# One lane of the odd steps' y is evicted by VectorE instead of ScalarE in a displaced-convolution kernel

## The reference

```python
def _gn(v, G=32, eps=1e-5):
    g = v.reshape(B_, G, C_ // G, H_, W_)
    m = jnp.mean(g, axis=(2, 3, 4), keepdims=True)
    s = jnp.var(g, axis=(2, 3, 4), keepdims=True)
    return ((g - m) / jnp.sqrt(s + eps)).reshape(v.shape)
...
disp = _displace(x.reshape(B, P, cpp, h, w), off_int)
d = field[None] + sub[:, None, None, :]
kernel = jnp.exp(-jnp.sum(d * d, axis=-1) / (2.0 * SIGMA ** 2))
kernel = kernel / jnp.sum(kernel, axis=(1, 2), keepdims=True)
out = lax.conv_general_dilated(disp, kw, padding=[(c, c), (c, c)], feature_group_count=C)
...
x = x + _L0_conv_ref(_gn(x), L0_conv_offset)
```

## Time and profile before

| | us |
|---|---|
| median of 3 runs | 1216.74 |
| lowest and highest run | 1216.17, 1218.03 |
| the profiled execution, device time | 1216.96 |
| its span, first to last instruction | 1215.1 |
| PE busy | 1169.8 (96%) |
| PEld busy | 1127.1 (93%) |
| DVE busy | 995.5 (82%) |
| ACT busy | 697.5 (57%) |
| POOL busy | 660.9 (54%) |
| mean granted TensorE clock | 0.996 |

### The profile page before, as it was taken

The page is one execution under the profiler, slowest core; times in us unless marked ns, Lnnn a source line. Parts: engine busy times, 40 slices in busy tenths (PEclk is TensorE's granted clock), DMA queues, the critical chain, the costliest instruction groups (busy, mean ns, idle before and its releaser), DMA issues.

```text
span 1215.1 us, 110760 instructions
## 1 busy us (share of the span) xinstructions
PE 1169.8 (96%) x49408; PEld 1127.1 (93%) x49408; DVE 995.5 (82%) x1530; ACT 697.5 (57%) x595; POOL 660.9 (54%) x1478
## 2 busy tenths in 40 slices
PE   2899999999999999999999999999999999999996
PEld 2899999999999999999999999999999999999996
DVE  7688788888888888788888878878888888878863
ACT  3455655656656565665665665565565566566553
POOL 5455555556565555655556555555655556564551
PEclk9899999999999999999999999999999999999999
DMA  9799999999999999999999999999999999999955
GB/s 311 248 321 334 347 347 344 343 342 345 344 338 342 346 349 345 341 344 345 346 341 346 344 336 349 340 347 344 341 347 339 347 339 350 343 344 343 336 182 185
DMA packets 409765, 403.01 MB, mean 332 GB/s; under 512 B 16528, under 2 KB 409744, under 8 KB 409744
## 3 DMA queue, kind: packets, MB, share of 16 engines
q1 hardware_dynamic: 204944, 201.41, 51.3%
q10 hardware_dynamic: 204800, 201.36, 49.4%
HBM read 201.38 MB, written 201.33 MB: 331 GB/s over the span
## 4 chain that ended last, share of the span: by engine, by line
PE 94%; DVE 2%; issue 2%; POOL 1%; DVEq 0%; POOLq 0%
PE ps L604 59%; PE ps L615 31%; PE ps L596 4%; DVE ay L425 1%; DVE xin L460 1%; POOL norm L294 0%; POOL t_int L232 0%; POOL t_full L238 0%; POOL grid_i L212 0%; DVE xin L463 0%; POOL var L281 0%; POOL rstd L283 0%; DVEq L423 0%; DVE sub L379 0%; DVE tap L341 0%
## 5 line engine op out<-in xcount | busy, mean ns | idle before, releaser
L604 PE MATMUL ps<-ay,norm 32*128 32x128 f32 x24576 | 728.0, 273 | 0.9 <-DVE both L448 0.3
L604 PEld LDWEIGHTS ps<-ay,norm 32*128 32x128 f32 x24576 | 704.6, 187 | 11.0 <-issue 0.7
L549 ACT ACTIVATE y<-ps 128x1536 f32<-128x1536 f32 x256 | 369.7, 1444 | 420.3 <-PE ps L604 420.1
L441 DVE BATCH_NORM_STATS2 stats<-xin 128x6 f32<-128x512 f32 x768 | 475.7, 689 | 0.1
L615 PE MATMUL ps<-ax,y 64*64 64x64 f32 x24576 | 419.4, 220 | 7.8 <-issue 7.6
L615 PEld LDWEIGHTS ps<-ax,y 64*64 64x64 f32 x24576 | 383.8, 135 | 29.6 <-issue 8.6
L294 POOL TENSOR_SCALAR norm<-xin,rstd,bias 128x768 f32<-128x768 f32 x256 | 264.1, 1032 | 211.1 <-PE ps L604 187.6
L463 DVE TENSOR_TENSOR xin<-ps,xin 128x1024 f32<-128x1024 f32 x256 | 312.7, 1222 | 45.7 <-PE ps L615 45.7
L540 ACT ACTIVATE norm<-xin,bias,rstd 128x768 f32<-128x768 f32 x256 | 262.9, 1028 | 73.8 <-issue 73.5
L460 DVE TENSOR_TENSOR xin<-ps,xin 128x512 f32<-128x512 f32 x256 | 175.6, 686 | 150.1 <-PE ps L615 150.1
L274 POOL TENSOR_TENSOR mean_sq<-both 128x4 f32<-128x4 f32 x128 | 25.5, 199 | 218.6 <-DVE both L448 198.2
(11 more groups left out here) (54 smaller groups left out, 188.2 us busy)
## 6 DMA issues: line engine op xcount, KB each, us to landing
xin<-in_x_dram SPq DMA_DIRECT2D x512, 384.0 KB, 5.6
out_dram<-xin ACTq DMA_DIRECT2D x512, 384.0 KB, 6.2
off<-in_L_conv_offset_dram SPq DMA_DIRECT2D x1, 48.0 KB, 3.4
```

The lines of the kernel that those rows point to most:

```text
L441: nc.vector.bn_stats(stats[:, s // PAIR % RING, s % PAIR, n, :], xin[:, s].rearrange("p (g q) f -> p q f g", g=GROUPS)[:, n]).then_inc(bn_ ...
L549: nc.scalar.activation(y[:, v].rearrange("p k r a m -> p a (k r) m"), ps[:, v, :, 0:POS * P].rearrange("p a (n m) -> p a n m", m=32), ACT. ...
L604: last = nc.tensor.matmul(ps[:, v, a, P * k:P * (k + 1)], norm[rows, v, r, P * k:P * (k + 1)], ay[rows, k, r, :], start=(r == 0), stop=(r ...
```

## The change

A new function `copy_last_lane` on VectorE copies lane 3 of the odd step's y (384 columns, one bank) from PSUM to SBUF, in every even step, ahead of that step's `add_x`; in step 14 it stands behind `swap_rows`. ScalarE's copy in odd steps is cut to the lanes 0 to 2 (1152 columns); in even steps it stays as it is. A new semaphore `last_lane_ready` tells TensorE, which now waits for it as well before `x_products(1)`.

```diff
+        last_lane_ready = sem("last_lane_ready")
...
+            def copy_last_lane(t):
+                dve.wait_ge(y_done, t + 1)
+                nc.vector.tensor_copy(y[:, 1].rearrange("p k r a m -> p a (k r) m")[:, LANES - 1],
+                                      ps[:, 1, LANES - 1, 0:POS * P].rearrange("p (n m) -> p n m", m=32)
+                                      ).then_inc(last_lane_ready, PAIR)
...
                 if s == STEPS - PAIR and not tail:
                     swap_rows(c + 1)
+                if s % PAIR == 0:
+                    copy_last_lane(t + 1)
                 for part in range(ADDS):
                     add_x(t, s, part)
...
             def copy_y(t, v, first):
+                lanes = LANES - v
                 act.wait_ge(y_done, t + 1)
                 if not first:
                     act.wait_ge(x_done, ADDS * (t - 1))
-                nc.scalar.activation(y[:, v].rearrange("p k r a m -> p a (k r) m"),
-                                     ps[:, v, :, 0:POS * P].rearrange("p a (n m) -> p a n m", m=32),
+                nc.scalar.activation(y[:, v].rearrange("p k r a m -> p a (k r) m")[:, 0:lanes],
+                                     ps[:, v, 0:lanes, 0:POS * P].rearrange("p a (n m) -> p a n m", m=32),
                                      ACT.Copy).then_inc(y_ready, 1)
...
                 pe.wait_ge(y_ready, two)
+                pe.wait_ge(last_lane_ready, one)
                 pe.sem_inc(x_started, 1)
                 x_products(1)
```

## The result

The changed kernel took 1227.19 us (median of four runs, 1226.46 to 1227.47) against 1217.22 us for the kernel before beside it. The ratio is 1.0075, with a 95% interval of 1.0062 to 1.0088, so 7.5 to 10.7 us slower; the two medians lie 10.0 us apart. The forecast was 1224.8 us, in a range of 1219.5 to 1235. The profiled execution is 1226.46 us with a span of 1224.6 us, 9.5 us above the span of before.

A forecast was written before the change was run, and what follows sets the result against it. TensorE, 94% of the chain, was taken as the bound, with VectorE's L460 gating `sum_stats`. Terms +7.05 + 1.2 - 0.2 = +8.05 us on 1216.74 gave 1224.8 us, range 1219.5 to 1235.

The forecast's parts named there:

- The gate: VectorE's L460 releases TensorE's `sum_stats` 0.15 us after its end in all 126 pairs, without slack.
- The copy's duration: VectorE's new copy of 384 columns from PSUM takes 552 ns, with ends of 0.35 and 0.69 us.
- rival B: VectorE's copy runs at the rate of copies in SBUF, 0.35 us, giving 1220.6 us; chance 0.10.
- The usual pair: In 96 pairs the copy runs from +0.14 to +0.69, covered with 0.16 us to spare: cost 0.
- Rival A: Cover in usual pairs too thin: copy starts later or takes longer, L460 0.08 us late, 1235.5 us; chance 0.17.
- The swap pair: In 15 pairs with `swap_rows` the copy queues ahead of L460, which starts 0.47 us later: +7.05 us.
- The pair behind `values`: In 15 pairs the copy starts behind L415 and delays L460 by 0.08 us: +1.2 us.
- ScalarE and the last pairs: ScalarE's shorter copy is off the path in 126 pairs and gains only in the last two: -0.2 us.
- C: ScalarE's copy gates `x_products(1)`; shortening it gives up to 0.11 us in 111 pairs, 1212.6 us; chance 0.06.
- D: VectorE's and ScalarE's reads of PSUM hold each other up, slowing L460; counted into the thin-cover rival, no own chance.

The follow-up runs named there:

- e5: The changed kernel with two lanes of the odd step's y copied by VectorE and two by ScalarE; 1269.61 us against 1216.98 for the kernel before.
- e7: The kernel before with part 0 of `add_x` cut in two in even steps, `sum_stats` waiting only for the first piece (lane 3); 1214.46 us against 1216.98.
- e2: The changed kernel without VectorE's copy in step 14 of superblocks 0 to 14, ScalarE copying all four lanes there; 1219.81 us against 1217.30 before.
- e3: The changed kernel with `swap_rows` moved behind `sums` in step 14; 1214.48 us against 1217.30 for the kernel before.
- e1: The kernel before with ScalarE copying only lanes 0 to 2 in odd steps and nobody copying lane 3; 1219.01 us against 1217.30.
- e8: The changed kernel with `swap_rows` moved behind `sums` and part 0 of `add_x` cut in two; 1211.91 us against 1216.98 for the kernel before.
- e4: The kernel before with `swap_rows` moved behind `sums` in step 14; 1211.49 us against 1217.30.
- e6: The changed kernel with VectorE's copy of the lane ahead of `swap_rows` in step 14; 1232.03 us against 1216.98 for the kernel before.

## Why the prediction was right, point by point

**The gate.** That L460 gates `sum_stats` in every pair was read from three equal distances of 0.15 us. It holds: 0.29 us of 0.31 us came through in e5, and the distance went away when the gate was moved (e7). What the prediction didn't see, and what its sum didn't need, is that the gate was costing only 0.01 us in a usual pair.

**The copy's duration.** 552 ns by the slope of L460 and L463; measured 557. The end of 353 ns (rival B) fell: a copy from PSUM doesn't run at the rate of copies within SBUF. 0.96 us for 768 columns and 0.56 for 384 make 1.04 ns a column. The rule of the Trainium skill, "VectorE: DVE Perf Modes", section "Why PSUM operands drop a tier", agrees with that; the estimate of 525 ns from the same page's cost table was 32 ns too low.

**The usual pair.** Covered, as forecast: L461 stays at +0.76. The cover was thinner than I had it. The copy starts at +0.20 and not +0.14, and ends at +0.76, so the spare time is 0.08 (L461 could have started 0.08 before the copy's end) and not 0.16. The start was taken from a single row of ScalarE in written-out code; the rows of the loop had +0.23 and +0.28. Rival A's condition, start + duration above 0.85, came to 0.76 and didn't hold.

**The swap pair.** Forecast 15 x 0.47 = 7.05 us. In the 14 looped ones L461 is 0.47 later, 6.5 us, and in superblock 0 `sum_stats` is 1.16 us later, 0.7 of it by the meeting with GpSimd. Sum 7.7 us. That the total came so close to e2's 7.4 us is in part luck, since e2 takes the copy away and keeps the 0.7; its wait for part 0 is 6.7 us shorter (15.0 to 8.3).

**The pair behind `values`.** Forecast 15 x 0.08 = 1.2 us; the mean over the 15 is 0.08 us more from `x_products(0)` to `sum_stats`, and it still stood there in e2 and e3.

**ScalarE and the last pairs.** Counted at -0.2 us. The last pairs' part of the profile, from the 126th `sum_stats` pair on, is 0.1 us shorter. Nothing else came of it (e1).

**What the sum lacked.** +8.05 us forecast; 9.5 in the profiled spans, and 7.5 to 10.7 by the runs, so the forecast lies inside. The terms for the swap pairs and for those behind `values`, 8.25 us in the forecast, came to 7.7 + 1.2 = 8.9, and the difference is the 0.7 us of superblock 0. Another 0.3 us lie ahead of the second pair. The rest lies in the y products, in two parts that work against each other. The block of 192 matmuls takes one of two lengths: from first to last start, 27 of 124 blocks are over 5.415 us before and 72 of 124 after, 2.4 us more in sum. On the other side, y begins late (over 0.152 us behind the last `x_products` matmul) in 41 pairs before and in 22 after, 1.7 us less in sum. What is left of the two is 0.7 us. e3, which has the change, has 26 long blocks and e4, which hasn't, 20, so VectorE's copy doesn't make the blocks long by itself. What makes a block take one length or the other was not tested and is open.

**The rivals.** A and B fell by the trace, and C by e1 and again by e8. D fell too: the two copies run side by side, and ScalarE's takes 1118 ns beside VectorE's and 1119 in e1, where VectorE copies nothing; VectorE's takes the 0.56 us of its slope.

## What to carry to other kernels

Before you hand an eviction to another engine, find out who waits for the one that it shortens, and what is queued behind the one that it adds. Here nobody waited for ScalarE's copy (0.33 us shorter, nothing gained), while the instruction behind the new copy on VectorE released TensorE with no slack. The copy was covered in 96 of 126 pairs, and the 30 others make up nearly 9 of the 9.5 us.

A distance that is the same in pairs with a real wait and in pairs without a listed one marked a gate here. It says what more lateness will cost, and not what the gate costs now; that took a run with the gate moved (e7). Moving the rare, long instructions (`swap_rows`) from ahead of it to behind it was worth 5.8 us, more than either division of the eviction that was tried, both of which cost time.

## What the runs showed of the hardware that I had not expected

A few hundredths of a microsecond decide which of VectorE's copies within SBUF and GpSimd's L295 is held up. Started 0.02 us ahead of L295, the three copies keep their 1.10 us and L295 stretches from 0.98 to 1.76; started behind it, they take 1.56 us and L295 keeps its 0.98; with L295 in between, 1.80 and 1.40. The order of two groups of VectorE instructions that wait for the same semaphore, the copy of y and `swap_rows`, is thus worth 5 to 6 us in this kernel (e6).

A gate that ends exactly when the waiting engine would be ready looks like a bottleneck from one side only: 0.31 us more lateness cost 0.29 us (e5), and a release 0.26 us earlier gained 0.01 (e7).
